# Self-attention of a four-layer gated network: output products issued ahead of a slot's scores on TensorE

## The reference

```python
q = jnp.einsum('bsc,hcd->bhsd', xn, wq)
k = jnp.einsum('btc,hcd->bhtd', yn, wk)
v = jnp.einsum('btc,hcd->bhtd', yn, wv)
a = jax.nn.softmax(jnp.einsum('bhsd,bhtd->bhst', q, k) * D ** (-0.5), axis=-1)
if causal:
    s, t = (a.shape[-2], a.shape[-1])
    mask = (jnp.arange(t)[None, :] > jnp.arange(s)[:, None]).astype(a.dtype)
    a = a * mask
o = jnp.einsum('bhst,bhtd->bhsd', a, v)
```

## Time and profile before

| | |
|---|---|
| time, median of 3 runs | 2252.91 us (2251.24 to 2258.19) |
| the profiled execution | 2261.2 us, its span 2259.5 us |
| mean granted clock of TensorE | 0.935 |
| busy over the span | PE 87%, PEld 67%, DVE 53%, ACT 41%, POOL 24% |
| the stage of the change | about 835 to 1310 us of the span |

### The profile page before, as it was taken

The page is one execution under the profiler, slowest core; times in us unless marked ns, Lnnn a source line. Parts: engine busy times, 40 slices in busy tenths (PEclk is TensorE's granted clock), DMA queues, the critical chain, the costliest instruction groups (busy, mean ns, idle before and its releaser), DMA issues. The chain is left out here.

```text
span 2259.5 us, 34056 instructions
## 1 busy us (share of the span) xinstructions
PE 1958.5 (87%) x12569; PEld 1503.3 (67%) x12569; DVE 1197.3 (53%) x2377; ACT 915.7 (41%) x1810; POOL 536.6 (24%) x958
## 2 busy tenths in 40 slices
PE   5995995567776979999999979969899889999997
PEld 4663884456644746666666668846588578888897
DVE  4873223425934628888888824457623542232232
ACT  4221001123343648888888823333333242222232
POOL 0012222131021522222222233211123132222222
PEclk9997995668988989999999999989999999999999
DMA  2005442000030692444443030210000335556584
GB/s 97 1 1 168 130 147 52 4 24 16 2 34 1 178 248 52 95 94 95 94 94 95 11 119 10 31 40 1 1 15 1 114 128 189 176 153 194 171 276 169
DMA packets 169668, 198.94 MB, mean 88 GB/s; under 512 B 43627, under 2 KB 139906, under 8 KB 163360
## 3 DMA queue, kind: packets, MB, share of 16 engines
q1 hardware_dynamic: 157840, 183.67, 27.6%
q0 software_dynamic: 10944, 13.03, 3.1%
q10 hardware_dynamic: 720, 0.07, 0.0%
HBM read 162.45 MB, written 36.70 MB: 88 GB/s over the span
## 5 line engine op out<-in xcount | busy, mean ns | idle before, releaser
L2969 DVE TENSOR_REDUCE l3s_mx<-banks 128x1 f32<-128x1024 f32 x256 | 308.3, 1215 | 28.7 <-PE banks L2868 28.1
L1285 PE MATMUL banks<-l3f_xrt,l3f_w 128*128 128x256 f32 (+1 forms) x1536 | 275.5, 340 | 1.5 <-issue 1.5
L2868 PE MATMUL banks<-l_stack 128*128 128x512 bf16 x1024 | 262.5, 381 | 10.1 <-PEq L44 9.8
L1285 PEld LDWEIGHTS banks<-l3f_xrt,l3f_w 128*128 128x128 f32 x1536 | 248.1, 191 | 26.9 <-issue 1.7
L1570 DVE TENSOR_SCALAR l3f_sg<-banks 128x256 f32<-128x256 f32 (+1 forms) x192 | 71.9, 375 | 280.0 <-PE banks L1285 280.0
L1352 ACT ACTIVATE l3f_sg<-l3f_sg 128x256 f32<-128x256 f32 (+1 forms) x192 | 72.3, 377 | 201.8 <-DVE l3f_sg L1570 201.8
L2960 ACT ACTIVATE x_features<-banks,l3s_mx 128x1024 f32<-128x1024 f32 x128 | 142.5, 1114 | 25.3 <-DVE l3s_mx L2969 23.7
L2868 PEld LDWEIGHTS banks<-l_stack 128*128 128x128 bf16 x1024 | 100.2, 98 | 77.9 <-issue 12.5
L2960 ACT ACTIVATE xn_tokens<-banks,l3s_mx 128x1024 f32<-128x1024 f32 x128 | 142.6, 1114 | 18.3 <-DVE l3s_mx L2969 18.2
L1298 PE MATMUL banks<-l3f_w,l3f_ht 128*128 128x256 f32 x624 | 138.5, 379 | 0.0
L2884 PE MATMUL banks<-ident,xn_tokens 128*128 128x128 f32 x832 | 120.5, 277 | 17.7 <-DVE l3s_pt L2932 9.9
(11 more groups left out here) (549 smaller groups left out, 3567.7 us busy)
## 6 DMA issues: line engine op xcount, KB each, us to landing
l3f_w<-in_L_ffn_gate_up_w_dram SPq DMA_DIRECT2D x24, 2048.0 KB, 8.3
l3f_w<-in_L_ffn_down_w_dram SPq DMA_DIRECT2D x24, 1024.0 KB, 7.7
l0f_w<-in_L_ffn_W_dram SPq DMA_DIRECT2D x16, 1024.0 KB, 8.0
l_stack<-l_q_part SPq DMA_DIRECT2D x64, 256.0 KB, 5.8
l_stack<-l_k_part SPq DMA_DIRECT2D x64, 256.0 KB, 11.2
l_q_part<-l_stack SPq DMA_DIRECT2D x24, 256.0 KB, 3.0
l_k_part<-l_stack SPq DMA_DIRECT2D x24, 256.0 KB, 3.7
l_values<-l3p_vs SPq DMA_DIRECT2D x16, 256.0 KB, 3.7
```

The source lines that it names most:

```text
L1285: last = nc.tensor.matmul(ps[:, f % 4, h * PAIR:h * PAIR + size(t)], w1_sb[:, p, dc, h * FF + f * P:h * FF + (f + 1) * P], xrt[:, p, dc, 0 ...
L2868: last = nc.tensor.matmul(ps[:, 2 * (v % SCORES) + h, :], stack[p][0][s][:, r, si * P:(si + 1) * P], stack[p][1][s][:, r, h * 512:(h + 1) ...
L2969: nc.vector.tensor_reduce(mx[:, v % RING:v % RING + 1], ps[:, 2 * (v % SCORES):2 * (v % SCORES) + 2, :].rearrange("p a n -> p (a n)"), AX_ ...
```

## The change

In PE's loop the call of `output` is moved from behind `scores(v)` to ahead of it. The other engines' loops, the numbering of the bank uses and all waits inside the functions stay as they are.

```diff
@@ -2905,10 +2905,10 @@
                     if v < ENTRIES * UNITS and v % UNITS == 0:
                         e = v // UNITS
                         pe.wait_ge(loaded[e % 2], 16 * LOADS * (e // 2 + 1))
+                    if v >= OUT and (v - OUT) % R == 0:
+                        output((v - OUT) // R)
                     if v < ENTRIES * UNITS:
                         scores(v)
-                    if v >= OUT and (v - OUT) % R == 0:
-                        output((v - OUT) // R)
                     if TURN <= v < ENTRIES * UNITS + TURN:
                         turn(v - TURN)
```

## The result

| | before | after |
|---|---|---|
| time, median (4 runs each) | 2255.55 us (2251.24 to 2261.45) | 2281.70 us (2278.31 to 2285.13) |
| ratio | | 1.0107, 95% interval 1.0088 to 1.0125 |
| span of the profiled execution | 2259.5 us | 2280.0 us |
| period of an entry in the stage | 58.83 us | 62.20 us |

A forecast was written before the change was run, and what follows sets the result against it. DVE, always working or waiting for PE, was taken to bound the changed stage. 31 pairs x (0.46 short + 0.53 long) = 31 us over the median 2252.9 gave 2284 us, range 2265 to 2308.

The forecast's parts named there:

- What bounds the stage: Layer 3 self-attention: DVE is always working or waiting for PE, 449.4 of 450 us, so longer waits lengthen the kernel.
- the 35.7 us: DVE's wait for PE before copying out an output tile (L2946), 850 to 1300 us; claimed to stay, not be won.
- Short output, 0.46 us: Short tiles' outputs: scores stand behind the waiting output, so the maximum starts 0.51 us later, less 0.05; 0.46 us each.
- start credit: Short outputs: how much earlier the output itself starts after the change; 0 to 0.13 us, taken as 0.05.
- Long output, 0.53 us: Long tiles' outputs start earlier, but scores behind them delay DVE's maximum, partly regained from vanished waits; loss 0.53 us each.
- without them the step from maximum to maximum is 1.48: Long output with eight chunks: DVE's step between maxima without its idle 0.40 and 0.57 us; gives a loss of 0.50.
- The prediction's last sign: Profile after: the prediction is wrong if DVE's three waits for PE together don't grow by about 31.
- only short outputs cost: Rival: DVE, already late, meets long outputs with scores in time, so 0.53 falls away; 14 us, 2267 us; chance 10%.
- each costs a whole block: Rival: PE sets the pace behind each output, so each costs 0.87 us of scores; 54 us, 2307 us; 10%.
- PE's lead: Rival at long outputs: lead grows from 1.73 to 3.2 us, both DVE waits vanish; 11 us faster, 2242; 5%.
- given back between outputs: Rival: exp on ACT, not DVE, sets the pace between outputs, so the lateness drowns there; 2253 us; 6%.
- The clock: Rival: PE's stops before short outputs lower its clock, at least 1 us each, adding 31; 2315 us or more; 3%.

The follow-up runs named there:

- short_to_act: Kernel before with only the copy of a short tile's output moved from DVE to ACT, PE's order unchanged; ratio 0.9980 to the kernel before, period 58.13 us.
- short_early: Kernel before with only the outputs of short tiles (w odd) moved ahead of the scores; ratio 1.0061 to the kernel before, period 60.81 us.
- long_early: Kernel before with only the outputs of long tiles (w even) moved ahead of the scores; ratio 1.0044 to the kernel before, period 60.18 us.
- after_act: Changed kernel's order on PE, with every output copied by ACT instead of some by DVE; ratio 1.0122 to the kernel before, period 62.19 us.
- half_long: Kernel before with, in slots of long outputs, the second half of the scores put behind the output; ratio 1.0058 to the kernel before, period 60.17 us.
- late1_act: Kernel before with long tiles' outputs one slot later, behind the scores, and all outputs copied by ACT; ratio 1.0006 to the kernel before, period 59.04 us.
- half_short: Kernel before with, in slots of short outputs, the second half of the scores put behind the output; ratio 1.0004 to the kernel before, period 59.08 us.

## Why the prediction was right

**What bounds the stage.** Right, and shown: DVE's work and its waits for PE again make up the whole of the stretch. That the 35.7 us were no prize is shown by short_to_act, where that wait is gone and its sum comes back elsewhere.

**Short output, 0.46 us.** It is 0.50 (short_early), or 0.48 as the mean of the four sizes in the trace of after: the maximum starts 0.52 us later behind L2901, less what the output starts earlier. The steps stand: that start credit is 0.12 with four chunks (0.27 less 0.15) and 0.04 in the mean of the four (0.05 predicted), scores start 0.16 behind L2901, the maximum 963.18 to 964.41 = 1.23 behind it (1.22 predicted), DVE's copy fits in the gap. The trace agrees with the Trainium skill, "TensorE: Matmul & The Clock Gate", Step-by-step: what each phase is for (matmuls keep program order): PE stands 0.63 to 0.86 us before the output in each of the 31 short slots of after, and in none do the slot's scores start ahead of it.

**Long output, 0.53 us.** The mechanism is right, the size too large: 0.34 (long_early) to 0.36 (the 0.84 us of a pair in the whole change less 0.48). The step that failed is "without them the step from maximum to maximum is 1.48". It measured 973.31 - 971.97 = 1.34. I had taken the idle time of the earlier trace rows out of the old step, as if instructions without a wait stood end to end. They overlap: the copy starts at 973.11, while the maximum is shown until 971.97 + 1.23 = 973.20, and the next maximum starts 0.08 ahead of the copy's end. So a wait that vanishes gives back its idle time and some 0.08 us of overlap, here twice. With 1.34 the working gives 1.34 - 0.87 - 0.11 = 0.36, which is what the stretches around such an output show in long_early (0.36). With five chunks it is further off: 0.57 predicted, 0.27 in long_early (0.40 and 0.35 with seven and six). There the step is 957.35 - 955.61 = 1.74 and not 1.88, again 0.14 less, and the row of two maxima in the earlier trace rows hides one more wait that goes away: it lasts 2.52 us there and 2.34 after.

```profile
955.61 1.22 DVE L2969 TENSOR_REDUCE l3s_mx<-banks 128x1 f32<-128x1024 f32 x1 [0.88 <-PE banks L2868]
956.75 0.68 DVE L2932 COPY l3s_pt<-banks 128x512 f32<-128x512 f32 x1
957.35 2.34 DVE L2969 TENSOR_REDUCE l3s_mx<-banks 128x1 f32<-128x1024 f32 x2
```

The scores of the second of these maxima, in the kernel before:

```profile
955.65 1.03 PE L2868 MATMUL banks<-l_stack 128*128 128x512 bf16 x4
```

That maximum starts at 955.41 + 2.52 - 1.22 = 956.71, 1.06 us behind them, so it waited for them, with 0.07 us of idle time that the row doesn't set apart and the overlap lost. 0.57 - 0.14 - 0.18 = 0.25 is near what was measured. That the maximum comes 1.4 us late with eight chunks was right (DVE waits 1.42).

**Sum.** 31 x (0.46 + 0.53) = 31 us was forecast, and the terms as measured give 31 x (0.50 + 0.34) = 26: the short one was 0.04 too low, the long one 0.19 too high. That 2284 lies only 2.3 us from the measured 2281.70 is in part luck: 31 us were 5 too many, and the median that they were added to, 2252.91, lies 2.6 below that of the four runs, 2255.55. DVE's waits for maxima rose to 50.0 us in 450 (some 55 predicted), the period to 62.20 (62.8 predicted). The prediction's last sign, DVE's three waits growing by about 31, came out at 26: they went from 61.0 to 82.3 us in the same 450 us, which is from 8.0 to 11.4 us an entry, for 31 pairs 26.

**Rivals.** That only short outputs cost, and that each costs a whole block, are refuted by short_early and long_early. PE's lead didn't grow: at the long output it is 971.97 - 970.90 = 1.07 us, against 1.06 for a maximum that waits for its scores. Nothing was given back between outputs, since the two parts measured alone add up to the whole. The clock stayed at 1.00 though PE stands 0.63 to 0.86 us before each short output. The rule of the Trainium skill, "TensorE: Matmul & The Clock Gate", A second HAM failure mode: psum-queue depth-cycling, isn't borne out by these stops.

**Left open.** Why single entries take some 0.15 to 0.2 us longer (one of before, two of after, two of after_act among others) wasn't followed up, nor why one entry of half_long took 61.32 us instead of 60.17, with PE standing 0.76 us inside an output, a stop for which the trace shows no releaser. The rest of late1_act's loss, beyond the stop ahead of the scores, is open too.

## What to carry to other kernels

In a queue worked in order, what stands ahead of an instruction that must wait is cover for that wait: before moving the waiting one forward, look at when its releaser ends, not at who waits for its result. A long wait in the table of waits is a prize only if its engine would not meet the same partner at its next instruction; giving the work to another engine is a quick test of that. And when a wait drops out of a chain, take starts from rows where the same instructions follow each other without one, not the old starts less the idle time. A merged row that lasts longer than its fellows can hide a wait.

## What the runs showed of the hardware that I had not expected

Consecutive DVE instructions without a wait between them overlap in the trace, mostly by 0.08 to 0.09 us (971.97 + 1.23 against 973.11; 973.11 + 0.28 against 973.31). The stage repeats to 0.02 us an entry, while whole executions of one kernel spread by 10 us: a period inside a trace told a change apart (0.25 us an entry in half_short) that twelve timed runs couldn't.
